# A gated attention and quantised FFN block on one core: gate factor multiplied apart, last down product in column halves, three PSUM banks for gate products and two for up products

## What is computed

```python
def _quant_weight(w):
    scale = jnp.mean(jnp.abs(w)) + EPS
    wq = jnp.clip(jnp.round(w / scale), -1.0, 1.0)
    return (wq, scale)
def _quant_act(x):
    s = jnp.max(jnp.abs(x), axis=-1, keepdims=True) / 127.0 + EPS
    xq = jnp.clip(jnp.round(x / s), -128.0, 127.0)
    return (xq, s)
...
gate = jax.nn.silu(_qlinear(x, w_gate))
up = _qlinear(x, w_up)
return _qlinear(gate * up, w_down)
...
x = x + jnp.tanh(g_xattn[0]) * xattn(ctx_512, ctx_512, masks, _layernorm(x), Wq, bq, Wk, bk)
x = x + jnp.tanh(g_ffn[0]) * ffn(_layernorm(x), w_gate, w_up, w_down)
```

## Time and profile before

| | |
|---|---|
| median of the runs | 224.27 us |
| the profiled execution, its own time | 224.45 us |
| its span on the core | 222.5 us |
| PE busy | 199.3 us, 90% |
| DVE busy | 180.2 us, 81% |
| ACT busy | 124.5 us, 56% |
| POOL busy | 97.8 us, 44% |
| moved by DMA | 32.84 MB |

### The profile page before, as it was taken

One profiled execution on the slowest core, in us unless ns is written; L12 is line 12 of the kernel. 1 busy time (PEld: TensorE's weight loads), 2 busy tenths in 40 slices (PEclk: granted clock), 3 DMA queues, 4 the chain that ended last, 5 costly groups with the idle time before them and its releaser, 6 DMA issues.

```text
span 222.5 us, 2846 instructions
## 1 busy us (share of the span) xinstructions
PE 199.3 (90%) x854; PEld 90.3 (41%) x854; DVE 180.2 (81%) x359; ACT 124.5 (56%) x165; POOL 97.8 (44%) x154
## 2 busy tenths in 40 slices
PE   8764008999999998999999999999999999999994
PEld 7221004344444344444444444444444444444441
DVE  0598979799989799797997989888898987888721
ACT  2179998999895952246964414896413035453000
POOL 2629743593764955320499204135973312020200
PEclk9995555899999999999999999999999999999999
DMA  6999999790022577300235640343607830540592
GB/s 215 420 423 423 417 391 424 281 325 8 3 47 47 115 186 172 98 0 3 47 64 121 153 91 15 69 80 74 141 3 175 201 89 13 96 79 16 97 188 94
DMA packets 47360, 32.84 MB, mean 148 GB/s; under 512 B 40944, under 2 KB 41072, under 8 KB 45808
## 3 DMA queue, kind: packets, MB, share of 16 engines
q1 hardware_dynamic: 47200, 32.51, 50.4%
q10 hardware_dynamic: 144, 0.13, 0.3%
HBM read 18.48 MB, written 4.19 MB: 102 GB/s over the span
## 4 chain that ended last, share of the span: by engine, by line
PE 71%; DMA 14%; ACT 5%; DVE 4%; issue 2%; SPq 2%; DVEq 0%
PE pU L947 23%; PE pG L934 23%; PE pD L965 20%; DMA stage_b<-in_L_ffn_w_up 8%; DMA stage_a<-in_L_ffn_w_down 4%; PE pA L909 3%; ACT down_w L689 2%; DMA stage_b<-stage_b 2%; ACT L736 1%; ACT hid L736 1%; DVE abs_part L1345 1%; SPq L351 1%; PE pA L898 1%; ACT stage_b L743 1%; DVE am L1320 1%
## 5 line engine op out<-in xcount | busy, mean ns | idle before, releaser
L736 ACT ACTIVATE hid<-pG,act_g 128x512 f32<-128x512 f32 x64 | 43.6, 688 | 54.6 <-PE pG L934 54.4
L934 PE MATMUL pG<-gate_w,xqT 128*128 128x512 f16 x256 | 64.7, 388 | 1.4 <-DVE xqT L1303 0.8
L947 PE MATMUL pU<-up_w,xqT 128*128 128x512 f16 x256 | 62.7, 379 | 0.0
L965 PE MATMUL pD<-down_w,stage_b 128*128 128x512 f16 x256 | 57.3, 379 | 0.6 <-DMA stage_b<-stage_b 0.6
L1311 DVE TENSOR_TENSOR hid<-pU,hid 128x512 f32<-128x512 f32 x64 | 43.6, 685 | 11.1 <-PE pU L947 9.2
L934 PEld LDWEIGHTS pG<-gate_w,xqT 128*128 128x128 f16 x256 | 25.1, 100 | 37.0 <-issue 8.0
L965 PEld LDWEIGHTS pD<-down_w,stage_b 128*128 128x128 f16 x256 | 24.9, 98 | 31.8 <-issue 2.3
L947 PEld LDWEIGHTS pU<-up_w,xqT 128*128 128x128 f16 x256 | 25.1, 98 | 31.3 <-issue 1.7
L743 ACT ACTIVATE stage_b<-hid,inv 128x1024 f16<-128x1024 f32 x15 | 16.9, 1139 | 7.8 <-DVE inv L1329 7.8
L560 POOL TENSOR_SCALAR out_scale<-den,act_e,down_k 128x1 f32<-128x1 f32 x16 | 5.9, 371 | 33.4 <-DVE den L1326 33.4
L909 PE MATMUL pA<-kT,qT 128*128 128x512 f32 x26 | 15.4, 678 | 4.9 <-ACT kT L709 4.9
(11 more groups left out here) (96 smaller groups left out, 236.1 us busy)
## 6 DMA issues: line engine op xcount, KB each, us to landing
stage_a<-in_L_ffn_w_gate SPq DMA_DIRECT2D x4, 1024.0 KB, 11.2
stage_b<-in_L_ffn_w_up SPq DMA_DIRECT2D x4, 1024.0 KB, 19.2
stage_a<-in_L_ffn_w_down SPq DMA_DIRECT2D x4, 1024.0 KB, 9.0
stage_b<-in_x SPq DMA_DIRECT2D x2, 1024.0 KB, 5.3
out<-x SPq DMA_DIRECT2D x8, 256.0 KB, 2.4
out<-stage_b SPq DMA_DIRECT2D x8, 256.0 KB, 2.4
ctx_s<-in_ctx SPq DMA_DIRECT2D x4, 256.0 KB, 14.4
x<-in_x SPq DMA_DIRECT2D x2, 512.0 KB, 5.8
```

Of the source, the lines that this page charges most:

```text
L736: act.activation(hid[:, t % NH, n * 512:(n + 1) * 512], pG[c % NG][:, :], ACT.Silu, scale=act_g[:, t:t + 1]).then_inc(silu_done, 1)
L934: ins = pe.matmul(pG[c % NG][:, :], xqT[:, t // TILES % 2, t % TILES, k, :], gate_w[:, n, k, :], start=k == 0, stop=k == KD - 1)
L947: ins = pe.matmul(pU[c % NU][:, :], xqT[:, t // TILES % 2, t % TILES, k, :], up_w[:, n, k, :], start=k == 0, stop=k == KD - 1)
L965: ins = pe.matmul(pD[t % ND][:, :], hidT[:, t % 2, k, :], down_w[:, k // KD, k % KD, :], start=k == 0, stop=k == KI - 1)
```

## The change

1. `NG, NU` go from 2, 3 to 3, 2: three banks for gate products, two for up products.
2. The factor 1/sum x tanh(g) is made by DVE for all tiles of a group at once. The multiplication of the softmax numerator by it becomes a call of its own, `gate_probs`, which a new table gives to ACT for nine tiles and to POOL for three; POOL's `residual1` keeps the addition.
3. The down product of tile 15 is made in two halves of 256 columns, each over all 16 inner blocks, the second one in the other `pD` bank. Each half has its own residual and its own store.
4. `k_copy(1)` and `k_copy(2)` go from ACT to DVE.
5. The tables and the order of all five engines' lists are new.

```diff
-NG, NU, ND = 2, 3, 2
+NG, NU, ND = 3, 2, 2
...
+        GATE_BY = "-P--APAAAAA-APAA"
+        CENTRE_BY = "PAPVAAAAPAPPVPVV"
+        QUANTISE_BY = "PAPPAAAPAVAPAVVA"
...
-        ABS_BY = ["AAAV", "AVAA", "AAAA"]
-        SIGN_BY = ["QXXX", "QQQX", "XXQQ"]
+        ABS_BY = ["AAVA", "AAAA", "AAAA"]
+        SIGN_BY = ["XQXQ", "QQXQ", "QXQX"]
...
+            def gate_probs(t):
+                probs_t = probs[:, t % NP, :]
+                pool.wait_ge(rgate_ready, group_of(t) + 1)
+                pool.tensor_scalar(probs_t, probs_t, rgate[:, t:t + 1], 1.0, ALU.mult, ALU.mult).then_inc(gated_pool, 1)
+
             def residual1(t):
...
+                who = GATE_BY[t]
+                pool.wait_ge({"A": gated_act, "P": gated_pool}[who], upto(GATE_BY, t))
+                pool.tensor_tensor(xt(t), probs[:, t % NP, :], xt(t), ALU.add).then_inc(x2_pool, 1)
...
+            def down_columns(t, half):
+
+                cols = slice(half * 256, half * 256 + 256)
+
+                bank = pD[(t + half) % ND]
+                pe.wait_ge(final_ready, t - ND + 1 + half)
+                for k in range(KI):
+                    if half == 0 and k % 8 == 0:
+                        pe.wait_ge(hidT_ready[t % 2][k // 8], 16 * (t // 2 + 1))
+                    ins = pe.matmul(bank[:, cols], hidT[:, t % 2, k, :], down_w[:, k // KD, k % KD, cols],
+                                    start=k == 0, stop=k == KI - 1)
+                ins.then_inc(down_half, 1)
...
+            def residual2_columns(t, half):
+                cols = slice(half * 256, half * 256 + 256)
+                dve.wait_ge(down_half, 2 * t + half + 1)
...
+            def k_copy(b):
+                dve.wait_ge(k_done, b + 1)
+                dve.tensor_scalar(kT[:, b % NQ, :], pA[:, :], bias_s[:, 1:2], None, ALU.add).then_inc(k_ready, 1)
```

More of the change, by code:

```diff
@@ L815, in _ @@
             silu(6, 0)
+            silu(6, 1)
+            quantise_hidden(4, 0)
+            silu(6, 2)
+            quantise_hidden(4, 1)
+            silu(6, 3)
+            silu(7, 0)
             exp(8)
@@ L1044, in _ @@
             down(2, 3)
-            pe.wait_ge(k_ready, 4)
-            score(8)
+            gate(4, 0)
+            up(4, 0)
+            gate(4, 1)
+            gate(4, 2)
+            up(4, 1)
             down(3, 0)
@@ L1103, in _ @@
             score(13)
+            up(7, 2)
             up(7, 3)
+            pe.wait_ge(scored, 14)
+            score(14)
             gate(8, 0)
@@ L1107, in _ @@
             gate(8, 1)
+            gate(8, 2)
             up(8, 1)
-            pe.wait_ge(scored, 14)
-            score(14)
-            gate(8, 2)
             up(8, 2)
@@ L1473, in _ @@
             inverse_hidden(3)
-            residual2(1)
-            stats2(5)
-            stats1(9)
             stats2(6)
-            absmax_x(5)
-            inverse_std2(2)
-            inverse_x(2)
+            reciprocal_scale(2)
+            stats2(7)
+            residual2(2)
             absmax_x(6)
-            residual2(2)
-            stats2(7)
+            inverse_std2(3)
+            absmax_x(7)
+            product(4, 0)
+            inverse_x(3)
+            product(4, 1)
             score(8)
-            reciprocal_scale(2)
@@ L1486, in _ @@
-            absmax_x(7)
+            absmax_hidden(4, 0)
             mask_and_max(8)
-            inverse_x(3)
+            residual2(3)
+            reciprocal_scale(3)
+            stats1(10)
             score(9)
-            residual2(3)
+            stats1(11)
             mask_and_max(9)
-            product(4, 0)
-            inverse_std2(3)
-            stats1(10)
-            product(4, 1)
+            stats1(12)
+            product(4, 2)
+            stats1(13)
+            product(4, 3)
@@ L1534, in _ @@
-            product(7, 1)
+            inverse_std2(4)
             inverse_x(4)
-            inverse_std2(4)
             stats2(10)
+            quantise_x(9)
             score(12)
-            centre(10)
-            mask_and_max(12)
+            reciprocal_scale(4)
             absmax_x(10)
             residual2(6)
-            reciprocal_scale(4)
+            mask_and_max(12)
             score(13)
+            residual1(11)
+            mask_and_max(13)
             product(7, 2)
-            mask_and_max(13)
+            stats2(11)
```

577 lines of the change are left out of this document (290 added, 287 removed).

## The result

The changed kernel takes **229.01 us** (median of 4 runs, 228.85 to 229.31) against 224.27 us before: the ratio on record is 1.0205, with a 95% interval of 1.0191 to 1.0219 (the two medians alone give 1.0211). It is slower by 4.7 us, where 2.4 were forecast. One execution of experiment 11, at a mean granted clock of 0.652, took 311.46 us and is left out of its ratio.

What follows compares the result with a forecast made beforehand. PE was taken as the bound from about 45 us on, so waits there add in full. Terms +0.2, +1.0, +1.6, 0 and -0.4 gave +2.4 on the profiled 224.45: 226.9 us, range 223.2 to 229.4.

Steps and rivals of the forecast that it cites:

- first gate product: On PE in the head: should start at about 31.4 us, 3.8 us earlier than before.
- third weight sum: On PE, behind the last down chunk's load and ACT's sum: comes at 48.0 to 48.8 us, 48.65 before.
- head, up to the third weight sum: Start to the last weight sum: most of the earlier start is lost; between -0.2 and +0.6, middle taken, +0.2 us.
- from there to 90 us: Weight sum to 90 us: new waits 1.85 and 0.5, less 1.35 of old ones, +1.0 us.
- 90 us to the last up product: PE waits for DVE's products ahead of up(9, 0), 0.7, and up(10, 2), 0.9: +1.6 us.
- gate factor: Factor made apart, nine multiplications moved from POOL to ACT: PE waits for neither in this stretch, 0 us.
- last down product and end: Tile 15's column halves: PE's time stays, shorter residual and store save; -0.4 us, bounds -0.3 and -0.6.
- the small waits: Before 90 us, three up products 0.95 us early together, counted half, 0.5; after 90 us, others find banks free.
- The cover named: For the moved gate multiplications costing 0: PE is 30 us behind these norms.
- rivals 1 and 2: Head start before 49 us: all 3.8 us kept, 221.9 us, chance 0.15; or half kept, 223.3 to 225.2, chance 0.21.
- rival 3: Idle PE ahead of score(7) and the weight sum drops the clock to 1.2 GHz for 5.6 us: 228.7 us, chance 0.15.
- the rival's cover: In the clock case, 1.0 us of the 2.8 lost that waits would have taken anyway.

Runs made afterwards that it cites:

- experiment 11: Changed kernel with two gate and three up banks, silu(1,3), silu(2,1) and gate(2,1) each moved earlier: 223.69 us, ratio 0.9956.
- Experiment 1: Kernel before, each up product from chunk 16 on waiting for the product two chunks back instead of three, as with two banks: 227.78 us, ratio 1.0146.
- experiment 3: Changed kernel with two gate banks and three up banks again, order and placement as changed: 224.64 us, ratio 1.0012.
- experiment 4: Changed kernel with product(8, 2) ahead of score(15) and product(10, 0) ahead of absmax_hidden(9, 1) on DVE: 226.97 us, ratio 1.0113.
- experiment 6: Changed kernel with silu(1,3) and silu(2,0) ahead of the second group's exponentials on ACT, gate(2,1) ahead of score(8) on PE: 227.75 us, ratio 1.0144.
- experiment 5: Changed kernel with the third weight sum behind gate(1,3) on PE and its reading behind product(1,0) on DVE: 228.55 us, ratio 1.0188.
- Experiment 9: Changed kernel with all gate products on POOL, none on ACT: 229.01 us, ratio 1.0197.
- Experiment 7: Kernel before with the gate factor made per group on DVE and the gate product of nine tiles on ACT, three on POOL: 226.50 us, ratio 1.0089.
- experiment 2: Kernel before with only the last down product, residual and store in two column halves: 223.94 us, ratio 0.9972.

## Why the prediction was right in sign and short in size

The steps of the prediction against the two profiled executions:

| step | forecast | measured |
|---|---|---|
| first gate product | 31.4 | 31.82 |
| third weight sum | 48.0 to 48.8 | 48.87 |
| head, up to the third weight sum | +0.2 | +0.6 |
| from there to 90 us | +1.0 | +1.6 |
| 90 us to the last up product | +1.6 | +2.7 |
| gate factor | 0 | 0 |
| last down product and end | -0.4 | -0.5 |
| sum | +2.4 | +4.4 of 4.5 |

**Right: the mechanism and its places.** After key projection 3 the forecast had waits of 0.9 and 0.95 us; they cost 0.94 (62.95) and 0.98 (65.75). Ahead of up(9, 0) and up(10, 2) it had 0.7 and 0.9; they cost 0.75 and 1.07. Experiment 1 makes the last two in the old order, experiment 3 takes away every wait for a product of DVE, and experiment 4 takes away the last two and wins close to their sum. The wait ahead of score(8) is not the ring's: experiment 3 leaves it at 0.78 us idle, and the new order around key projection 3 makes it (experiment 6).

**Mis-sized: the small waits.** "Such small ones I count half, 0.5", and behind 90 us "other up products find their bank free by my count". From 49 to 90 us PE's starts show 0.20 (57.08), 0.60 (60.27) and 0.13 (72.80) lost beside the two large waits, 0.9. From 90 us on seven rows beside up products start 0.09 to 0.20 late, 0.9 together, where the sum had none. This is 0.4 and 0.9 of the shortfall of 2.1; the two large waits there are another 0.2 longer than forecast. In experiment 3 none of those behind 66 us is left: they belong to the ring as well.

**Mis-sized: the head.** The weight sum came at 48.87, just behind the late end of the range, 48.8, and the term 0.4 over the value taken from its middle: +0.22 in its start, +0.86 for one unit less ahead of it, -0.45 for the transposes already done, 0.6. The bound of the last gate chunk ended at 42.0, forecast 40.6 to 41.4. Part of that late end goes with a clock that fell, which is told below: in experiment 4, whose program is the same up to there and whose clock held, the sum stood at 47.95, which by the same count is -0.3, just ahead of the early end. So the bounds were right to 0.1 us either way, and which of them is met goes with the clock, which the sum didn't have. The first gate product, forecast at 31.4, is right in part by luck: it came at 31.82 with that fall, and at 30.67 in experiment 4 and 30.48 in experiment 5 without it.

**Right: the columns.** 32 matmuls of 256 columns took 3.66 us from the first's start, and the unit rule for 16 of 512 gives 3.62. Half a residual took 0.48 for 0.75, 0.27 less as forecast, and from the start of the last residual to the end of the span are 2.65 us against 3.15: with the 0.04 of PE's time, -0.46. The step worked out from the rows held: (3.66 - 0.17) / 32 is 0.109 us, forecast 0.108. "TensorE: Matmul & The Clock Gate", Back-to-back issue gap, in the Trainium skill has 81 ns for a pair of weight load and matmul of 128 columns in a stream, 25 more than the row; carried over to 256 columns, an estimate, that would have been 0.8 us more, and the trace doesn't show it. The same section of the Trainium skill has a formula for a lone matmul, columns / 2.4 + 2.5 ns, which gives 109 ns for 256 columns; with that one the trace agrees. The trace disagrees with "ScalarE: Activation LUTs", What ACT_TABLE_LOAD costs, in the Trainium skill: in ACT's order of time of the kernel after, the silu starts 1.30 us after the start of the load, where the page has 2.66 for load and drain. The load alone agrees, 1.28 us in both:

```profile
62.91 1.28 ACT L753 ACT_TABLE_LOAD   x1
64.21 1.27 ACT L753 ACTIVATE hid<-pG,act_g 128x512 f32<-128x512 f32 x2
```

**Right here, and not in general: the factor at nothing.** The cover named was that PE is 30 us behind these norms. Experiment 9 agrees with the nothing for this order. Experiment 7 shows that the cover named was not enough: the norms can wait, but other steps stand behind the moved product. One is a silu behind it in ACT's own list, and 0.72 us ahead of the wrong silu reached PE in full. The other is a quantisation in POOL's list, behind the addition that waits for the product. The prediction gave 0.7 us for a step of ACT in front of an addition; here POOL waited 3.64 us for it, and PE 1.12. The order of the change puts the products elsewhere.

**The rivals.** The head start was not kept (rivals 1 and 2): experiment 5 shows that a pause taken out of the head comes back as a wait for a product. The clock did not fall again in the kernel after (rival 3): every window from 37.0 us on is at the 2.4 GHz level. It did in the profile of experiment 9, after 1.94 us of idle PE ahead of score(7), where the rival had placed it. Windows of that kernel (length, busy PE, PEld, DVE, ACT, POOL, granted clock, DMA share, GB/s):

```profile
42.00:43.00 1.00, 0.00 (x0) 0.00 (x0) 0.96 (x4) 0.58 (x1) 1.00 (x1) 1.00 0.92 147
...
44.00:45.00 1.00, 1.00 (x3) 0.24 (x2) 0.80 (x3) 0.99 (x3) 1.00 (x1) 0.66 1.02 426
45.00:46.00 1.00, 1.00 (x4) 0.31 (x3) 0.75 (x1) 0.00 (x0) 1.00 (x2) 0.50 0.81 254
```

It was short there, until about 47.6, not the 5.6 us of the rival. By its own words the rival's cover left out makes 224.45 + 2.4 + 2.8 = 229.65, not the 229.4 at which the range ends; and the gains of 1.5 to 2.3 us of the second rival make 223.4 to 224.2, not up to 225.2.

**What the split of the banks costs.** Between the changed kernel and experiment 3 lie 4.4 us of medians. They are not all the ring's: all four executions of the changed kernel had a mean granted clock of 0.955, nine of the twelve of experiment 3 had 0.962. Three of experiment 3 had 0.954 and took 225.26 to 225.70, so at a like clock the split costs 3.3 to 3.8 us; experiment 1 gives 3.3 in the other order. That the rest, about 0.9, is chance of the clock and not a part of the change is what the runs point to, not what they show: no execution of the changed kernel itself had the higher clock.

## What to carry to other kernels

When PSUM banks are dealt out between two rings, ask how late each ring's consumer can be, not how busy it is: the bank taken from DVE's ring, whose list holds scores and reductions of 1.2 us between the products, cost 3.3 us, while all that the bank given to ACT's ring could win in the old order were two waits for a silu, 0.5 us together. They are this row of PE's waits in the kernel before, from 30 us on:

```profile
PE pG L934 <- ACT hid L736: 0.5, 2, 0.4
```

A wait in the thick of the work was worth its full length where nothing near it was short (experiment 4), and only a part or nothing where the next product was late too (experiments 6 and 5). A step given to an engine that is 56% busy was free in one order here and cost 2 us in another (experiments 9 and 7): look at what stands behind it in that engine's list, and at what stands behind the step that waits for it in the other engine's list, not at the share.

## What was not expected of the hardware

**The clock fell while PE was working.** In the profiled execution of the changed kernel the granted clock went to its lower level, 1.2 GHz, at about 9.6 us and back at 13.0, in the middle of scores, on a part of the program that runs alike in other kernels. Windows of the kernel after, and then of experiment 5 with the same program there:

```profile
10.00:11.00 1.00, 1.00 (x2) 0.47 (x2) 0.11 (x1) 0.00 (x0) 0.00 (x0) 0.50 1.01 418
...
13.00:14.00 1.00, 1.00 (x4) 0.42 (x3) 1.00 (x4) 0.60 (x2) 0.00 (x0) 1.00 1.00 418
```

```profile
10.00:11.00 1.00, 1.00 (x4) 0.40 (x3) 0.96 (x4) 0.00 (x0) 0.00 (x0) 1.00 1.00 418
```

Four matmuls took 3.05 us (10.64) in the first and 1.88 in the second (at 9.26), and the first gate product came at 31.82 and 30.48. Ahead of the fall PE had been idle for 0.84 and 0.78 us between short pieces. The same two idle times stand in experiments 4 and 9, where the clock held there; what makes it fall in one execution and not in another stays open.

**The executions of one kernel fall into two groups by their mean granted clock.** In experiment 5, three with 0.962 took 227.95 to 228.35 us and three with 0.955 took 228.75 to 229.22; in experiment 4, 226.12 to 226.55 and 227.39 to 227.66; in experiment 6, 227.07 to 227.53 and 227.97 to 228.37. The step is 0.7 to 1.1 us, as large as many an edit here. By it, experiment 4 wins 1.6 us against the changed kernel (227.4 to 227.7 against 228.9 to 229.3, all at 0.955), against 1.8 for its two waits and 2.0 by the medians; experiment 6 wins 1.0, and experiment 5 nothing. By it, too, the three executions of experiment 3 at 0.954 stand at the 225.4 that was expected. In the old order two such groups, 0.946 and 0.954, overlap (experiment 2: 223.35 to 224.11, and 223.73 to 224.16).
